# Attention on one core: the masked scores' weights loaded in halves, and each pair's state update placed right behind its masked product

## What is computed

```python
q = _phi((x @ W_Q.T).reshape(b, t, H, DK))        # _phi(u) = elu(u) + 1
k = _phi((x @ W_K.T).reshape(b, t, H, DK))
v = (x @ W_V.T).reshape(b, t, H, DK)
def step(carry, inp):
    S, z = carry
    qt, kt, vt = inp
    S = g4 * S + jnp.einsum('bhi,bhj->bhij', kt, vt)
    z = g3 * z + kt
    num = jnp.einsum('bhij,bhi->bhj', S, qt)
    den = jnp.sum(z * qt, axis=-1, keepdims=True) + EPS
    return ((S, z), num / den)
_, ys = jax.lax.scan(step, (S0, z0), (qT, kT, vT))
gate = jax.nn.sigmoid(x @ W_g_w.T + W_g_b).reshape(b, t, H, DK)
y = (outputs * gate).reshape(b, t, H * DK)
return y @ W_O.T
```

## Time and profile before

| | us |
|---|---|
| median of 3 runs | 1033.98 |
| lowest and highest | 1030.67, 1035.63 |
| the profiled execution | 1030.6 |
| its span in the profile | 1028.8 |

### The profile page before, as it was taken

How to read it: one execution, slowest core, us unless ns; L and a number is a source line. 1 busy time by engine, 2 the same in 40 slices (tenths; PEclk the granted TensorE clock), 3 DMA queues, 4 the chain that set the end, 5 groups by cost and what they waited for, 6 DMA issues and landing times. The chain is left out here.

```text
span 1028.8 us, 24712 instructions
## 1 busy us (share of the span) xinstructions
PE 883.3 (86%) x8764; PEld 749.9 (73%) x8764; DVE 551.7 (54%) x1617; ACT 449.5 (44%) x957; POOL 477.5 (46%) x501
## 2 busy tenths in 40 slices
PE   4999999999999832998667779999986999999991
PEld 2787778777777731877564569999885679999991
DVE  4665666566665543655438958455385822222226
ACT  5535354353544200655327647533323544444444
POOL 3234343533435434677766400015604176767774
PEclk9999999999999875999979999999997999999996
DMA  7778500000000001333250001000005013322245
GB/s 248 256 277 329 208 17 5 21 8 13 13 8 20 22 19 52 103 103 101 60 165 2 2 3 23 3 4 3 1 2 207 11 55 88 94 79 88 87 119 164
DMA packets 72918, 79.28 MB, mean 77 GB/s; under 512 B 14429, under 2 KB 56676, under 8 KB 72320
## 3 DMA queue, kind: packets, MB, share of 16 engines
q1 hardware_dynamic: 61744, 59.69, 18.2%
q0 software_dynamic: 9216, 16.84, 4.8%
q10 hardware_dynamic: 1872, 1.58, 0.5%
HBM read 32.46 MB, written 47.77 MB: 78 GB/s over the span
## 5 line engine op out<-in xcount | busy, mean ns | idle before, releaser
L436 POOL TENSOR_TENSOR attn_qd<-attn_qT,attn_qpow 128x512 f32<-128x512 f32 x32 | 54.5, 1702 | 154.5 <-DVE attn_qT L726 154.5
L1465 ACT ACTIVATE routed_hT<-routed_hid,routed_B 128x256 f32<-128x256 f32 x160 | 65.8, 471 | 81.0 <-PE routed_hid L1388 81.0
L1034 POOL DMA_INDIRECT mixed<-moe_outs,moe_target x80 | 77.8, 972 | 38.4 <-DVE moe_outs L1136 16.2
L1306 POOL DMA_INDIRECT results<-routed_outs,routed_target x80 | 78.5, 981 | 28.3 <-issue 16.6
L1291 POOL DMA_INDIRECT queue_in<-routed_XN,routed_slot x64 | 64.0, 1000 | 47.1 <-DVE routed_slot L1566 22.2
L1400 PE MATMUL routed_outp<-routed_W,routed_hT 128*128 128x128 f32 x640 | 77.8, 275 | 0.0
L1388 PE MATMUL routed_hid<-routed_cols,routed_W 128*128 128x256 f32 x320 | 75.8, 380 | 0.5 <-DVE routed_cols L1614 0.5
L1400 PEld LDWEIGHTS routed_outp<-routed_W,routed_hT 128*128 128x128 f32 x640 | 74.7, 192 | 0.1
L595 PE MATMUL attn_av<-attn_v,attn_a 128*128 128x65 f32 x512 | 64.2, 280 | 9.3 <-DVE attn_a L737 8.9
L595 PEld LDWEIGHTS attn_av<-attn_v,attn_a 128*128 128x128 f32 x512 | 61.5, 196 | 13.4 <-DVE attn_a L737 12.7
L426 POOL DMA_INDIRECT sorted_rows<-attn_sent_rows,attn_slot x56 | 55.9, 998 | 18.3 <-issue 14.3
(11 more groups left out here) (332 smaller groups left out, 2275.2 us busy)
## 6 DMA issues: line engine op xcount, KB each, us to landing
sorted_rows<-attn_vacant SPq DMA_DIRECT2D x8, 2080.0 KB, 7.4
moe_rows<-sorted_rows SPq DMA_DIRECT2D x44, 130.0 KB
queue_in<-attn_empty SPq DMA_DIRECT2D x8, 645.0 KB, 7.1
routed_rows<-queue_in SPq DMA_DIRECT2D x40, 129.0 KB, 2.3
results<-attn_zero SPq DMA_DIRECT2D x8, 512.0 KB, 7.8
ssm_turn_buf<-mixed SPq DMA_DIRECT2D x16, 256.0 KB, 3.7
routed_W<-m1w SPq DMA_DIRECT2D x2, 2048.0 KB, 10.4
xs<-x SPq DMA_DIRECT2D x8, 256.0 KB, 4.4
```

The source lines that it names most:

```text
L436: pool.tensor_tensor(wide(of_pair(qd, p)), wide(of_pair(qT, p)), qpow[:, p * P:(p + 1) * P].unsqueeze(1).to_broadcast([P, BATCH, P]), ALU. ...
L1034: pool.indirect_dma_start(results, bass.IndirectOffsetOnAxis(target[:, n:n + 1], 0), outs[q][:, j * P:(j + 1) * P], None, bounds_check=2 * ...
L1306: pool.indirect_dma_start(results, bass.IndirectOffsetOnAxis(target[:, n:n + 1], 0), outs[t % KEPT_BACK][:, j * P:(j + 1) * P], None, boun ...
L1465: last = act.activation(hT[t % 2][:, m * GROUP:(m + 1) * GROUP], banks[q % 4][:, (m % 2) * GROUP:(m % 2 + 1) * GROUP], ACT.Silu, bias=B1[: ...
```

## The change

It has three parts, all in the attention phase. `values` loads the 128 columns of each weight tile in two halves of 64 and multiplies each with the same 65 columns of values, into the lower and the upper 64 partitions of `av`: 16 matmuls for 8. `new_state` of a pair comes right behind its own `values`, no longer behind the next pair's `carried`, and `kept_state` behind its own `divided`. And some waits and small groups move with them: `counted` goes from behind `queries_keys` to the end of pair 1, the wait for the sort's sums from the `new_state` of pair 1 in the old count to pair 2, and `combined` of pair 0 waits for one more `kept_state`.

```diff
@@ new_state
                 pe.wait_ge(s["kd"], at(i, 4, p + 1))
+                pe.wait_ge(s["state"], at(i, 4, p + 4))
+                if p == 1:
+                    pe.wait_ge(s["res"], at(i, 1, 1))
+                if p == 2 and places:
+                    pe.wait_ge(s["put"], at(i - 2, PLACED, SUMS_READ))
                 if p == 3 and sorts:
                     pe.wait_ge(s["sort"], at(i - 1, SORT_STEPS, LOGITS_READ))
-                if p == 1 and places:
-                    pe.wait_ge(s["put"], at(i - 2, PLACED, SUMS_READ))
-                if p == 0:
-                    pe.wait_ge(s["res"], at(i, 1, 1))
-                else:
-                    pe.wait_ge(s["state"], at(i, 4, p + 4))
@@ values
-                        mm = pe.matmul(av[:, h * 512 + b * (DK + 1):h * 512 + (b + 1) * (DK + 1)],
-                                       a[:, h * WIDE + b * P:h * WIDE + (b + 1) * P], v4[:, b, 2 * p + h, :],
-                                       start=False, stop=True, skip_group_check=True)
+                        for rows in (slice(0, P // 2), slice(P // 2, P)):
+                            first = h * WIDE + b * P
+                            mm = pe.matmul(av[rows, h * 512 + b * (DK + 1):h * 512 + (b + 1) * (DK + 1)],
+                                           a[:, first + rows.start:first + rows.stop], v4[:, b, 2 * p + h, :],
+                                           start=False, stop=True, skip_group_check=True)
@@ PE's step
-                if not first and not (last and p):
-                    new_state(*ahead_of, sorts, places)
...
                 values(i, p)
+                if not last:
+                    new_state(i, p, sorts, places)
                 if ahead:
                     values_gates(*target(i, p))
...
+                if p == 1 and places:
+                    if last:
+                        pe.wait_ge(s["res"], at(i, 1, 1))
+                    else:
+                        pe.wait_ge(s["state"], at(i, 4, 6))
+                    counted(i - 2)
...
                 if p == 0 and not first:
-                    pe.wait_ge(s["state"], at(i, 4, 4))
+                    pe.wait_ge(s["state"], at(i, 4, 4 if last else 5))
                     combined(i - 1)
@@ DVE's step
-                if not first and not (last and p):
-                    kept_state(*ahead_of)
                 masked(i, p)
...
                 divided(i, p, (lambda k: feature(*target(i, p), k)) if ahead else (lambda k: None))
+                if not last:
+                    kept_state(i, p)
```

More of the change, by code:

```diff
@@ L627, in step @@
                     queries_keys(*target(i, p))
-                if p == 1 and places:
-                    if last:
-                        pe.wait_ge(s["res"], at(i, 1, 1))
-                    else:
-                        pe.wait_ge(s["state"], at(i, 4, 5))
-                    counted(i - 2)
                 if p == 3 and sorts:
```

## The result

The changed kernel takes 1007.75 us (median of 4 runs, 1007.38 to 1008.22), the kernel before, timed beside it, 1034.81 us (4 runs, 1030.67 to 1035.77): a ratio of 0.9746, 95% interval 0.9719 to 0.9774. The forecast was 1013 us, in a range of 1007 to 1025. The profiled execution took 1007.95 us, with a span of 1006.1.

The account below looks back on a forecast made before the run. Attention was taken as bound by the ring of PE and DVE, with `values` on both ways. Savings of 4 x 2.2 + 3.0 + 2.7 + 2.6 + 3.9 = 21.0 us leave 1009.6; plus 3.4 gives 1013 us, range 1007 to 1025.

Parts of the forecast that it names:

- What attention saves, the span saves: Attention phase: it ends before the next phase can begin, so its saving, 21.0 us in sum, shortens the span.
- A pass of 29 ns, 1.55 us for `values` and `new_state`: PE, each pair: 48 half passes at 29 ns plus 0.16 of edges, 1.55 us against 2.36, saving 0.81.
- rival in which the halves don't overlap at all: `values`: a 64-column pass takes 109 ns like a whole one, `values` 3.5 us, the kernel about 1093; chance 0.05.
- Change of form 0.07 us: PE, from `outputs_turned` to `values`: one new change of form costs about 0.07 us, leaving 0.75 saved where PE is late.
- the loss of a whole record each time: PE, changes of tiling mode: 0.28 us lost at each of some 35 added ones takes 10 us back, giving 1022.
- Pair 1's wait: Chunk 4, before pair 1's `values`: PE now stands 1.0 to 1.1 us, with `scores` to `values` 5.7 us.
- Pair 1 to 2, saved 0.55: Chunk 4: DVE's way loses 0.79, 0.2 goes to `normalize` and `gated`, PE waits 0.5; 0.55 us saved of 10.16.
- Chunks 2 and 7: Attention's chunks 2 and 7: savings of 2.6 and 3.9 us, the latter with 1.6 from pair 2's half-clock `values`.
- better: One of two clock falls in chunks 2 and 7 goes, or a pass takes 27 ns: 1009 us; chance 0.08.
- the new waits cost clock: Chunks 3 to 6, pair 1's wait: half clock loses 1.7 us a fall; four falls give 1020, more 1025; chance 0.20.
- From the profile to the median: Whole kernel: the median of three runs lies 3.4 us above the profiled execution, so 1009.6 becomes 1013 us.
- the edges are paid once: PE, each pair: `new_state` follows `values` in the same form, so 0.16 us of edges counts once in 1.55.

Follow-up runs that it names:

- experiment 3: Changed kernel with the loop over the halves outermost, so 8 products of one half follow one another: 1028.12 us, ratio 0.9966 to the kernel before.
- the halves alone: Kernel before with only `values` split into two 64-column halves, the order of work kept: 1007.57 us, ratio 0.9758.
- experiment 2: Changed kernel with `values` whole again (128 columns), so the new order alone: 1033.5 us, ratio 1.0008 to the kernel before.
- experiment 6: Changed kernel with pair 1's `masked` ahead of `moments` and `slots_of` put off to pair 3: 1007.82 us; with `chosen` also moved to the next chunk: 1000.22 us.
- Quarters: Changed kernel with each 128-column product of `values` in four products of 32 columns, 64 a pair: 1006.6 us, ratio 0.9764 to the kernel before.
- experiment 7: Statistics (`moments`) put off behind pair 1's `kept_state`: with experiment 6's three moves 1014.02 us; with only pair 1's `masked` moved early 1032.28 us.

## Why the prediction was right, and where it was off

The mechanism and the sign were right, and the time lay in the range, 5.3 us below the forecast. That it lay so near is in part luck, as the paragraph on the median says. Its steps in turn:

**What attention saves, the span saves**: right. 25.3 us in attention, 22.7 in the span, the difference within the scatter of the rest.

**A pass of 29 ns, 1.55 us for `values` and `new_state`**: exactly what was measured. The picture behind it, 29 ns a pass as `new_state` and the 64x64 products have it, held since those alternate between two tiles as well; experiment 3 has the same products without the alternation, 57 ns a pass. The rival in which the halves don't overlap at all had 109 ns a pass and 1093 us. Without overlap a pass of half the columns took 57, and that kernel, beyond the turning point of 50 ns, came out at 1028.

**Change of form 0.07 us**: measured 0.10 (`outputs_turned` to `values` takes 0.53 us from start to start, 56.48 - 55.95, where it took 0.43). A second one was left out, from `new_state` to `values_gates`, whose first group takes 0.99 us for 0.95. A pair of chunk 0 saved 0.66 us for the forecast 0.75. The Trainium skill (TensorEngine Tiling (Array Packing), Key Properties) has a drain at every change of the tiling mode; the loss of a whole record each time, which the prediction priced at 1022 us, did not appear.

**Pair 1's wait**: forecast 1.0 to 1.1 us, measured 0.96. From `scores` to `values` it is 198.70 - 192.99 = 5.71 us, forecast 5.7. Pair 0 to 1 saved 0.24, forecast 0.2. Pair 3 to 0 saved 0.80, forecast 0.79; pair 2 to 3 0.67, forecast 0.65.

**Pair 1 to 2, saved 0.55**: this is the one term of chunk 4 that was mis-sized; it saved 0.89. I let PE wait 0.5 us for `masked` there and it waits for nothing. VectorE's way was shorter than I summed: its first operation for the weights took 0.64 us before and 0.25 us after, since `kept_state` now stands between it and the features. The operation ends 0.02 to 0.03 us after GpSimd's product for the queries, at 215.39 behind 215.36 before, at 203.53 behind 203.50 with the halves alone (0.64 us), at 202.76 behind 202.74 after; in the last the product ran nearly to its end beside `kept_state`. I had carried the 0.64 over as the operation's own length. That is 0.35 us in each of the chunks 3 to 6, 1.4 of the miss, and it moves with the order.

**Chunks 2 and 7**: forecast 2.6 and 3.9, measured 4.71 and 5.81. In both a stretch at half clock is gone, the ones that in the kernel before began at 110.9 and 329.4 us. I had that under "better", with one of the two and a chance of 0.08; both went, about 2 us each. A third that I had not listed went too, 3.4 us from 363.5, and pair 3 saved 0.9 more than forecast. The stretch of 6.8 us behind pair 2's wait is in both kernels, from 349.9 before and from 326.7 after. There the forecast was too high: the half form gave back 1.54 us (`values` takes 1.93 for 3.47, start to start; forecast 1.6), but the sum counts pair 2's `values` a second time with 0.75, and pair 2 to 3 saved only 0.91. Chunk 7 thus saved 2.4 us more than forecast in pair 0 to 1, 0.9 more in pair 3 and 1.4 less in pair 2.

**Rival "the new waits cost clock"**, chance 0.20: not in the changed kernel, whose four waits of 0.60 to 0.99 us all passed at full clock, in two profiles. It is real all the same: experiments 2 and 6 show it once each, at 1.6 us. My argument that one instance of 1.0 us had cost clock was as weak as I said.

**From the profile to the median**: I added 3.4 us, because the profiled execution of before was its fastest. The changed kernel's was 0.2 above its median. Of the 5.3 us, 3.6 come from here, and 1.7 from the sum of the steps against the spans (21.0 for 22.7). But that is luck: attention itself saved 26.0 us, 5.0 more than the sum (2.1 in chunk 2, 1.9 in chunk 7, 1.5 in 3 to 6, less 0.5 in 0 and 1), and scatter hid 3.4 of them, the later start of 0.7 and the 2.7 behind attention.

**What part 2 is worth**: I did not give it a number of its own. Its one gain in a pair where TensorE is late was in part 1's sum, "the edges are paid once"; experiment 2 shows it, 0.15 us a pair. With the halves the order is worth 2.9 us up to chunk 7, 0.2 to 0.6 a chunk; without them it costs, 0.3 in chunk 4; in the times neither can be seen.

## What to carry to other kernels

A product whose weights fill all 128 columns and whose moving side is as short as 65 started one pass every 112 ns; split by columns and issued in turn to the two halves, it took 0.98 us for 1.73. The sequence is the change: the same halves one after the other gave nothing.

When an engine is late over a whole stretch, moving one of its operations moves the wait with it. First list that engine's gaps, with their lengths, and move into a gap only what fits into it (4.1 us of `chosen` into 3.9, which gave about 7 us over either kernel without that move); what already lies in part in a gap, as the statistics did, costs when it is moved out (chunk 4 took 42.1 us for 40.4). And list what the other engines do in their own order behind it: GpSimd's had a part in both moves that failed (experiments 6 and 7).

## What I had not expected of the hardware

Quarters ran four at a time, 16 ns a pass, in the same rounds of about 57 ns as the halves. The Trainium skill (TensorE: Matmul & The Clock Gate, Wait — 56ns, not 53.3ns?) says of matmuls back to back that their starts never come closer than about 25 ns. Here, on different column groups, the starts within a round are 6 to 8 ns apart and the mean is 16, so that figure does not carry over to such products.

VectorE's operations and GpSimd's tensor operations hold each other up, and which of the two loses hangs on which began first. In the changed kernel's chunk 4 the same line of VectorE in pairs 1 and 2, and the product that GpSimd ran beside it:

```profile
200.97 0.64 DVE L727 SCALAR_TENSOR_TENSOR attn_kT<-attn_e,attn_r 128x512 f32<-128x512 f32 x1
...
210.48 1.63 DVE L727 SCALAR_TENSOR_TENSOR attn_kT<-attn_e,attn_r 128x512 f32<-128x512 f32 x1 [0.16 <-ACT attn_r L293]
```
```profile
201.02 1.72 POOL L436 TENSOR_TENSOR attn_qd<-attn_qT,attn_qpow 128x512 f32<-128x512 f32 x1 [2.55 <-DVE attn_qT L727]
...
210.29 1.27 POOL L436 TENSOR_TENSOR attn_qd<-attn_qT,attn_qpow 128x512 f32<-128x512 f32 x1 [5.50 <-DVE attn_qT L727]
```

In pair 1 VectorE began 0.05 us ahead and took 0.64 us, and the product took 1.72. In pair 2 the product began 0.19 us ahead and took 1.27, and VectorE took 1.63. All 32 pairs of this profile fall on one side or the other: 25 like the first (0.64 to 0.69 us, the product 1.63 to 1.73), 7 like the second (1.54 to 1.63, the product 1.27). Some small operations of VectorE that meet such a product end only behind it: in experiment 7 one on 128x4 (L797) took 0.85 us, for 0.17 in the changed kernel, and ended 0.03 us behind it. Not all are: `y` and `kept_state`, which read the banks `av` and `stp`, ran beside the product of pair 1 in their usual 0.69 and 0.48 us. What the two contend for was not tested.
